# Local attention on one core: the probabilities-times-values matmuls and three ScalarE steps take another place in the software pipeline

## What is computed

```
q, k, v = split(x @ Wqkv)                 # 16 heads of 64
q, k    = l2norm(q) * qs, l2norm(k) * ks  # then rotary tables on both
sim     = (q_window . k_two_windows) * 8  # windows of 32 tokens, own and previous
attn    = softmax(where(mask, -max, sim))
out     = attn @ v_two_windows
x       = out @ Wo + x
x       = (a * gelu(gate)) @ W2 + b2 + x  # feed-forward on layernorm(shift(x))
```

## Time and profile before

| | |
|---|---|
| runs (3) | 2629.06 us median, 2627.81 to 2631.6 |
| profiled execution: first to last instruction (span) | 2628.3 us; the page gives no other time of its own for it |
| TensorE matmuls | 2396.4 us busy, 91% of the span |
| TensorE weight loads | 1259.7 us, 48% |
| VectorE | 1953.7 us, 74% |
| ScalarE | 1795.4 us, 68% |
| GpSimd | 1082.1 us, 41% |
| mean granted TensorE clock | 0.971 |
| data moved | 29.92 MB, 11 GB/s on the mean |

### The profile page before, as it was taken

One profiled execution on the slowest core, in us unless ns is written; L12 is line 12 of the kernel. 1 busy time (PEld: TensorE's weight loads), 2 busy tenths in 40 slices (PEclk: granted clock), 3 DMA queues, 4 the chain that ended last, 5 costly groups with the idle time before them and its releaser, 6 DMA issues. The chain is left out here.

```text
span 2628.3 us, 62460 instructions
## 1 busy us (share of the span) xinstructions
PE 2396.4 (91%) x24940; PEld 1259.7 (48%) x24940; DVE 1953.7 (74%) x2595; ACT 1795.4 (68%) x2593; POOL 1082.1 (41%) x461
## 2 busy tenths in 40 slices
PE   7799999999999999999999999999999877767778
PEld 2355555555554555555545455555555422222355
DVE  5678777788677777787778777788777658999542
ACT  4677767777677776777767777677677666545533
POOL 0354444444444444444444444444444204556130
PEclk8899999999999999999999999999999989999989
DMA  0100000000000000000000000000000010000001
GB/s 21 54 2 2 2 26 10 10 2 2 15 22 11 2 2 14 22 11 2 2 14 14 19 2 2 14 14 15 5 2 2 2 37 0 0 0 0 18 23 41
DMA packets 16047, 29.92 MB, mean 11 GB/s; under 512 B 3616, under 2 KB 6064, under 8 KB 15664
## 3 DMA queue, kind: packets, MB, share of 16 engines
q1 hardware_dynamic: 15760, 25.78, 3.1%
HBM read 24.73 MB, written 1.05 MB: 10 GB/s over the span
## 5 line engine op out<-in xcount | busy, mean ns | idle before, releaser
L709 POOL TENSOR_TENSOR f_rot<-f_raw,f_tabc 128x1024 f32<-128x1024 f32 x192 | 452.6, 2357 | 694.7 <-DVE f_qk L757 302.4
L713 POOL TENSOR_TENSOR f_rot<-f_rot,f_shuf 128x1024 f32<-128x1024 f32 x192 | 453.1, 2360 | 470.0 <-DVE f_shuf L750 470.0
L607 ACT ACTIVATE f_raw<-f_ps 128x1024 f32<-128x1024 f32 x192 | 196.5, 1023 | 324.9 <-PE f_ps L431 324.9
L478 PEld LDWEIGHTS f_ps<-f_ptz,f_v 64*64 64x64 f32 x6144 | 260.2, 133 | 93.7 <-issue 93.7
L478 PE MATMUL f_ps<-f_ptz,f_v 64*64 64x96 f32 (+1 forms) x6144 | 286.7, 243 | 1.5 <-ACT f_ptz L628 1.4
L776 DVE TENSOR_REDUCE f_sum<-f_ps 128x8 f32<-128x512 f32 x192 | 131.8, 686 | 185.6 <-ACT f_ps L663 185.5
L747 DVE STREAM_SHUFFLE f_shuf<-f_raw 128x1024 f32<-128x1024 f32 x192 | 255.2, 1329 | 0.0
L757 DVE SCALAR_TENSOR_TENSOR f_qk<-f_rn,f_rot 128x1024 f32<-128x1024 f32 x192 | 233.5, 1216 | 28.8 <-POOL f_rot L713 28.8
L430 PE MATMUL f_ps<-f_xs,f_wq 128*128 128x512 f32 x384 | 220.7, 657 | 24.3 <-DVE f_xs L728 21.0
L750 DVE TENSOR_TENSOR f_shuf<-f_shuf,f_tabs 128x1024 f32<-128x1024 f32 x192 | 236.7, 1233 | 7.6
L616 ACT ACTIVATE f_rn<-f_ps 128x1024 f32<-128x1024 f32 x192 | 198.8, 1035 | 39.5 <-PE f_ps L437 39.0
(11 more groups left out here) (267 smaller groups left out, 3961.4 us busy)
## 6 DMA issues: line engine op xcount, KB each, us to landing
e_w<-in_e_w SPq DMA_DIRECT2D x16, 256.0 KB, 2.8
f_wq<-in_f_wq SPq DMA_DIRECT2D x12, 256.0 KB, 2.8
f_wk<-in_f_wk SPq DMA_DIRECT2D x12, 256.0 KB, 3.2
f_wv<-in_f_wv SPq DMA_DIRECT2D x12, 256.0 KB, 3.4
f_wo<-in_f_wo SPq DMA_DIRECT2D x6, 512.0 KB, 3.1
f_w<-in_f_w SPq DMA_DIRECT2D x6, 341.0 KB, 3.1
s_dx<-in_k_pick SPq DMA_DIRECT2D x1, 1536.0 KB, 9.3
f_w<-in_f_w SPq DMA_DIRECT2D x6, 192.0 KB, 3.8
```

Source lines behind the costliest of these rows:

```text
L478: mm = pe.matmul(view(ps, 7 * CH + 64 * p, [1, n], p0=64 * h, rows=64), v[64 * h:64 * h + 64, p * CH + 64 * j:p * CH + 64 * j + 64], ptz[6 ...
L709: pool.tensor_tensor(view(rot, 0, [S, 4], [1, S]), view(raw, 0, [S, 4], [1, S]), view(tab_c, 0, [S, 2], [0, 2], [1, S]), ALU.mult).then_in ...
L713: pool.tensor_tensor(rot[:, :], rot[:, :], shuf[:, :], ALU.add).then_inc(sem["rot"], 1)
```

## The change

TensorE does mix directly behind the scores in every slot. ScalarE does out_copy first, then the exponential, then raw_copy with its square, then value_copy; spread and inverse_norm keep their places. No instruction is added or removed; no buffer, semaphore count or duration changes.

```diff
 # TensorE, slot()
                 if run:
                     scores(i, j)
+                if had2:
+                    mix(u2, b2)
                 if before and j == 2:
                     wo_part(k, 6, 8)
...
-                if j == 6 and had2:
-                    mix(u2, b2)
                 if has:
                     if j == 7:
                         values(u, a)
                     project(u, a)
                     if j != 7:
                         values(u, a)
-                if j != 6 and had2:
-                    mix(u2, b2)
 # ScalarE, slot()
+                if had2:
+                    out_copy(u2, b2)
+                if run:
+                    need(act, sem["shift"], i * 8 + j + 1)
+                    act.activation(..., ACT.Exp, scale=8.0).then_inc(sem["exp"], 1)
                 if has:
                     raw_copy(u, a)
...
-                if has and j == 5:
-                    value_copy(u, a)
-                if run:
-                    need(act, sem["shift"], i * 8 + j + 1)
-                    act.activation(..., ACT.Exp, scale=8.0).then_inc(sem["exp"], 1)
-                if has and j != 5:
+                if has:
                     value_copy(u, a)
...
-                if had2:
-                    out_copy(u2, b2)
                 if had1:
                     spread(u1, b1)
```

More of the change, by code:

```diff
@@ L653, in slot @@
                     nc.scalar.preload_act_table_set(ACT_SET)
+                if had2:
+                    out_copy(u2, b2)
+                if run:
+                    need(act, sem["shift"], i * 8 + j + 1)
+                    act.activation(view(ps, 4 * CH, [CH, 2], [64, 4], [1, 64]), view(s[j % 2], 0, [64, 2], [128, 4], [1, 64]),
+                                   ACT.Exp, scale=8.0).then_inc(sem["exp"], 1)
                 if has:
@@ L658, in slot @@
                     act.activation(sq2[:, :], cen[:, :], ACT.Square).then_inc(sem["sq2"], 1)
-                if has and j == 5:
-                    value_copy(u, a)
-                if run:
-                    need(act, sem["shift"], i * 8 + j + 1)
-                    act.activation(view(ps, 4 * CH, [CH, 2], [64, 4], [1, 64]), view(s[j % 2], 0, [64, 2], [128, 4], [1, 64]),
-                                   ACT.Exp, scale=8.0).then_inc(sem["exp"], 1)
-                if has and j != 5:
+                if has:
                     value_copy(u, a)
```

## The result

The changed kernel takes 2745.78 us, the median of four runs (2744.38 to 2748.2); beside it the kernel before took 2629.98, so the ratio is 1.0443 [1.0431, 1.0456]. The profiled span grew from 2628.3 to 2744.2 us, by 115.9; the forecast sum was 96. The mean granted clock is 0.971 in both.

The account below looks back on a forecast made before the run. TensorE's instruction list was taken to set the time. Terms summed to +4.2 us per iteration: 92 over 22 looped iterations, 3.4 in iteration 23; 2628.3 + 96 = 2724, with the median 0.8 above: 2725 us, range 2670 to 2800.

Parts of the forecast that it names:

- the likeliest case: The forecast itself, chance 0.57: slower by 4.2 us per iteration, 2725 us, own range 2700 to 2750.
- Step 1: Gap between projection and norms: without mix TensorE stands 0.76 us in slots 2, 4 and 5, 0.91 in slot 7.
- Step 2: Exponential before the copy: slot 3's wait of 1.01 us ends, but norms wait 1.15 there and 1.6 in slot 5.
- the rival in which VectorE stays late: Slots 3 and 5: VectorE as late as before, so copies start late; +7.3 us per iteration, 2795 us, chance 0.1.
- Step 3: Mix behind the scores has its own semaphore waits: +0.18 us in slots 2 and 6, 0.03 in the others.
- Step 4: Slot 6: shifted input no longer late, but the GELU takes its place; -0.1 us, between -1.3 and +0.5.
- the prediction's own signs of being wrong: L436 shows no wait, the loss sits in slot 6, or single instructions have become slower on TensorE.
- Busy times: Sign expected in the changed profile: busy times of all engines stay.
- Step 5: ScalarE's out_copy first: the copy behind it is not later, and only the next slot's mix needs it; costs nothing.
- The clock rival: Behind slot 5's wait the clock falls to 1.2 GHz: 3.4 us more per iteration, 2800 us, chance 0.03.
- The faster rival: TensorE's two waits (54.6 us) go and no new one comes: 2574 us, chance 0.05.

Follow-up runs that it names:

- the filled gap: The changed kernel with the first four of the eight value matmuls done twice in slots 2, 4 and 5: 2730.35 us, ratio 1.0393.

## Why the prediction was right, step by step

The forecast was slower, 2725 us in 2670 to 2800; 2745.78 lies in it, and the likeliest case is what happened. The total is nearer than its parts: errors of both signs partly cancel, which is luck.

- *Step 1, mix leaves the gap.* Shown. The norms stand 0.77 in slots 2 and 4 (forecast 0.76), and the filled gap gives that back as free work. In slot 7 they start 0.94 later into the slot (7.88 against 6.94), as forecast. Slots 0 and 1, and slot 3 once its copy stands first, have them 0.44 after the transposes: no wait, as forecast. In slot 6 it is 0.47; there the square is only just done.
- *Step 2, exponential ahead of the copy.* Shown for slot 5: the norms start at 7.55 (7.7 forecast, 9.2 by the rival in which VectorE stays late), L824 runs in 0.69, and putting the order back gains 0.68. Slot 3 came out even (forecast +0.15), its norms starting at 8.02 (8.2). It takes both halves, since the exponential alone gives 7.48; the forecast did reckon slot 3 from a slot 2 whose mix was early. The path is the forecast one: the sine product of slot 2 is held by GpSimd's L705 and ends 1.09 after it, as in the earlier trace rows, and then L722 runs beside GpSimd's L709:

```profile
1171.57 2.36 POOL L705 TENSOR_TENSOR f_rot<-f_raw,f_tabc 128x1024 f32<-128x1024 f32 x1 [6.37 <-ACT f_raw L605]
1173.09 1.93 DVE L746 TENSOR_TENSOR f_shuf<-f_shuf,f_tabs 128x1024 f32<-128x1024 f32 x1
...
1175.16 2.36 POOL L709 TENSOR_TENSOR f_rot<-f_rot,f_shuf 128x1024 f32<-128x1024 f32 x1 [1.23 <-DVE f_shuf L746]
1175.65 2.15 DVE L722 TENSOR_SCALAR f_xs<-y_t 64x512 f32 x1
```

- *Step 3, mix's own wait behind the scores.* Forecast 0.18 in slots 2 and 6 and 0.03 elsewhere. In the median mix starts 1.41 after L450 in slot 2, as the earlier trace rows said, but 1.42 in slot 4, which was to be nearly free of it, and 1.58 in slot 6, twice the 0.18. Three semaphores are thus not the whole reason.
- *Step 4, slot 6.* **The mis-sized term**: -0.1 was taken, +0.58 came, just above the upper bound of +0.5. The text named the mechanism (the shift's wait goes, the GELU takes its place), but gave the GELUs' delay hardly a price. The projection starts 5.84 into the slot where the kernel before had it at 5.22 (1150.19 less 1144.97):

```profile
1144.97 0.38 PE L450 MATMUL f_ps<-f_maskb,f_identb 128*128 128x256 bf16 x2
...
1150.19 1.12 PE L430 MATMUL f_ps<-f_xs,f_wq 128*128 128x512 f32 x2 [0.58 <-DVE f_xs L728]
```

  The run with mix put back shows what the step cost: 1.25 in the slot (12.47 to 11.22), against the 0.67 that the early exponential gives (11.89 to 11.22). A loss in slot 6 was one of the prediction's own signs of being wrong; it came in part.
- *Busy times.* Said to stay; VectorE's rose by 53 us (1953.7 to 2006.4 on the page). The sine product takes 68 more: 100 of its 192 last over 1.5 us, where 2 did before, and each of the 100 began while GpSimd was at work; of the 92 short ones one did. The scaling takes 28 less, being no longer held:

```profile
L746 DVE TENSOR_TENSOR f_shuf<-f_shuf,f_tabs x192: 1224/1907/1991, 90.1 to 2175.1; 128x1024 f32<-128x1024 f32 x192
```

```profile
L824 DVE TENSOR_TENSOR f_xn<-f_cen,f_sq x24: 691/692/693, 223.8 to 2216.9; 128x512 f32<-128x512 f32 x24
```

- *Step 5, out_copy first.* Nothing, as forecast, as long as mix is early; without that it holds all of ScalarE.
- One term was missing: after a wait L436 lasts 0.96 to the start of L437, not the 0.86 of the earlier trace rows. With five waits an iteration (slots 2, 3, 4, 5 and 7, where four were forecast; slot 3's is the one that took the place of p's) that is 0.5, and slot 6, just in time, has it too.
- *The clock rival.* The clock kept its upper level behind slot 5's wait, as forecast, but the rows set against this rival do not bear that out. The waits of 5.3 and 2.4 us in the earlier trace rows ended at 82.35 and 2074.95 us, ahead of the loop and at its end, and behind both the granted clock was 0.50:

```profile
82.35:85.90 3.55, 3.55 (x4) 1.14 (x4) 0.92 (x4) 0.00 (x0) 0.00 (x0) 0.50 0.00 0
2076.00:2079.20 3.20, 3.20 (x50) 2.91 (x41) 1.38 (x2) 0.66 (x2) 0.00 (x0) 0.50 0.02 5
```

  The chance given to this rival thus rested on a reading that the rows do not bear out; that it failed is in this respect luck.

Slot 6 (+0.68 beside the forecast), slots 2 and 4 (+0.38), and the rest (-0.6) make the 0.5 between 4.2 and 4.70. The faster rival needed the square within 2.46 us of the key matmuls' start; in slot 4 L436 starts 3.22 after L431 (1191.34 less 1188.12), as the earlier trace rows said. Its prize was real: with the exponential early in two slots alone, the two waits fell from 54.6 to 20.9 us and the kernel gained 41.

## What to carry to other kernels

Before moving a group of work out of a gap between a producer and the step that needs its result, price the round trip through the other engine from a place in the trace where the gap is bare; the group may have been the cover. Moved ahead of the producer, it delays the whole chain behind it as well. And when two reorderings come together, try each place by itself: here one piece, in two slots, gains 1.5%, and the whole loses 4.4%.

## What the hardware showed that was not expected

In the run with ScalarE's half alone the granted clock falls behind the norms' waits. TensorE stood 2.63 us ahead of the norms in slots 2, 4 and 5 of each looped iteration, and windows around slot 2's show what followed:

```profile
1283.20:1285.90 2.70, 0.08 (x1) 0.00 (x0) 1.97 (x5) 2.67 (x5) 1.05 (x1) 1.00 0.00 0
1285.90:1289.10 3.20, 3.19 (x4) 1.13 (x5) 3.13 (x4) 1.42 (x4) 1.97 (x2) 0.56 0.00 0
```

Granted 1.00 while it stood, then a mean of 0.56, close to the lower level of 1.2 GHz; L436 and L437 took 1.52 and 1.71 from start to start instead of 0.96 and 0.86. It came after 45 of the 66 such waits in the looped iterations 1 to 22. After the same run's 44 waits of about 1.75 in slots 3 and 7, and after all of the change's looped norms' waits, up to 1.29 us, the matmuls kept their pace.

The clock falls in the other two kernels as well, at another place. At the start of every second iteration, once per pass of the loop, TensorE stands in the middle of the scores for something that the profile does not show. The change's list of waits has these ten stands, and a window shows what followed the one from 1231.32 to 1233.01:

```profile
PE f_ps L457 <- issue: 15.0, 10, 2.0
```

```profile
1234.40:1237.60 3.20, 3.20 (x19) 2.05 (x16) 2.84 (x5) 1.09 (x2) 0.00 (x0) 0.50 0.02 5
```

The clock fell behind 8 of these 10, and in the kernel before behind 9 of 10 (1.4 to 2.1 us, 18.0 in all). The shortest stand with a fall lasted 1.23 us; the 44 of 1.75 above had none. So the length of a stand alone does not tell whether the clock falls. The change hardly touches this cost, and the prediction, which counted two waits, had left it out.

The Trainium skill, TensorE: Matmul & The Clock Gate, section "HAM oscillation — how this bites in real kernels", warns of such a fall between bursts of matmuls; its example has longer waits, for transfers. These runs agree with the warning, and show it for shorter stands, so the measurement goes beyond the example. The clock rival was thus a real mechanism; none of the change's looped norms' waits brought it about.
